# Variance of four chunks as four 32-column products, roots on 128 partitions, the low part on GpSimd, and a share of one scaling on ScalarE

## The reference

```python
x = x + _L0_conv_ref(_gn(x), ...)   # masked, float32
x = x + _L1_conv_ref(_gn(x), ...)   # masked, left and right rounded to bfloat16
x = x + _L2_conv_ref(_gn(x), ...)   # no layer norm ahead, 16 channels
x = x + _L3_conv_ref(_gn(x), ...)   # no mask
```

```python
xn = layernorm(x, norm_g, norm_b)
m = mask[..., None]
left = xn @ Wl.T * m * jax.nn.sigmoid(xn @ Wlg.T)
right = xn @ Wr.T * m * jax.nn.sigmoid(xn @ Wrg.T)
out_gate = jax.nn.sigmoid(xn @ Wog.T)
out = jnp.einsum('bikd,bjkd->bijd', left, right)
out = layernorm(out, out_norm_g, out_norm_b) * out_gate
return out @ Wout.T
```

## Time and profile before

| | |
|---|---|
| median of three runs | 2122.47 us (2121.59 to 2125.39) |
| the profiled execution, its own time | 2120.04 us |
| its span in the profile | 2118.1 us |
| mean granted PE clock, share of full speed | 0.959 |
| busy in the span | PE 1768.2, DVE 1489.3, ACT 1344.1, POOL 805.5 us |
| `project` of layers 0, 1 and 3, gate sigmoids of first to last chunk | 98.4 to 357.2, 697.3 to 967.0, 1536.8 to 1800.9 us |
| `output` of layer 3, first to last scaling | 1970.0 to 2107.4 us |

### The profile page before, as it was taken

How to read it: one execution, slowest core, us unless ns; L and a number is a source line. 1 busy time by engine, 2 the same in 40 slices (tenths; PEclk the granted TensorE clock), 3 DMA queues, 4 the chain that set the end, 5 groups by cost and what they waited for, 6 DMA issues and landing times. The chain is left out here.

```text
span 2118.1 us, 40561 instructions
## 1 busy us (share of the span) xinstructions
PE 1768.2 (83%) x10305; PEld 1040.4 (49%) x10389; DVE 1489.3 (70%) x3176; ACT 1344.1 (63%) x2413; POOL 805.5 (38%) x740
## 2 busy tenths in 40 slices
PE   0899996797998999965599799799799997799665
PEld 0445444685553444443255477644345444688332
DVE  7688886125753999995977388466489899344775
ACT  0587884455995787854599566478487876244322
POOL 0045445005990344445699300089000000000799
PEclk9999998998998999998899899999899999899999
DMA  7367776774995355546399666199456867653799
GB/s 322 132 199 231 246 237 208 284 313 155 365 366 179 121 173 181 175 138 236 132 347 367 234 221 206 43 327 393 150 181 213 263 214 222 248 238 158 258 358 336
DMA packets 326944, 496.13 MB, mean 234 GB/s; under 512 B 22827, under 2 KB 188462, under 8 KB 320438
## 3 DMA queue, kind: packets, MB, share of 16 engines
q1 hardware_dynamic: 326838, 494.93, 68.0%
HBM read 285.12 MB, written 197.13 MB: 228 GB/s over the span
## 5 line engine op out<-in xcount | busy, mean ns | idle before, releaser
L1327 POOL TENSOR_TENSOR shared<-O,out_rs 128x128 f32<-128x128 f32 (+1 forms) x128 | 92.1, 722 | 676.5 <-DVE out_rs L1227 675.5
L601 PE MATMUL ps<-w_heads,hi 64*128 64x256 f16 x3072 | 291.2, 272 | 39.5 <-DVE sig L752 27.2
L664 ACT ACTIVATE sig<-ps,largest 128x512 f32<-128x512 f32 x384 | 247.3, 692 | 51.5 <-PE ps L601 49.6
L1104 ACT ACTIVATE O<-ps 128x512 f32 (+1 forms) x144 | 151.7, 1053 | 189.2 <-PE ps L1025 189.2
L645 ACT ACTIVATE zs<-ps,shift 128x512 f32<-128x512 f32 x192 | 131.8, 686 | 183.3 <-PE ps L569 183.2
L601 PEld LDWEIGHTS ps<-w_heads,hi 64*128 64x128 f16 x3072 | 154.4, 94 | 187.5 <-DVE sig L752 71.5
L1371 PEld LDWEIGHTS ps<-ident,shared 128*128 128x128 f32 (+1 forms) x1024 | 118.8, 134 | 235.9 <-POOL shared L1327 141.5
L1371 PE MATMUL ps<-ident,shared 128*128 128x128 f32 (+1 forms) x1024 | 162.7, 284 | 79.3 <-POOL shared L1327 79.2
L601 PE MATMUL ps<-w_heads,lo 64*128 64x256 f16 x1536 | 212.7, 271 | 0.0
L569 PE MATMUL ps<-xs,center 128*128 128x512 f32 x384 | 202.3, 609 | 11.7 <-DVE r_terms L716 5.4
L752 DVE SCALAR_TENSOR_TENSOR sig<-ps,largest,sig 128x512 f32<-128x512 f32 x256 | 179.6, 742 | 38.0 <-ACT sig L664 36.5
(11 more groups left out here) (163 smaller groups left out, 3642.1 us busy)
## 6 DMA issues: line engine op xcount, KB each, us to landing
shared<-left_right SPq DMA_DIRECT2D x34, 2048.0 KB, 12.1
shared<-gate SPq DMA_DIRECT2D x224, 256.0 KB, 4.5
gate<-gates SPq DMA_DIRECT2D x96, 512.0 KB, 2.9
x_dram<-shared SPq DMA_DIRECT2D x192, 256.0 KB, 4.3
shared<-x_dram SPq DMA_DIRECT2D x192, 256.0 KB, 4.4
xs<-x_dram SPq DMA_DIRECT2D x64, 512.0 KB, 4.2
left_right<-stage SPq DMA_DIRECT2D x64, 448.0 KB, 5.7
left_right<-shared SPq DMA_DIRECT2D x64, 448.0 KB, 5.8
```

What stands on the lines that cost most here:

```text
L601: last = pe.matmul(PAIR[row][:, g, kb * S:kb * S + S], tokens[half, q % 8, at:at + P], k["w_heads"][half, part, :], start=(step == 0), sto ...
L664: act.activation(sig[:, slot, :].rearrange("p (c e) -> p c e", c=4), pair(row, 0), ACT.Sigmoid, scale=k["largest"][:, 0:1]).then_inc(c["si ...
L1104: act.activation(o_of(ch), ps[h % 4 // 2][:, h % 2, :].rearrange("p (b g i) -> p b g i", b=2, g=2), ACT.Copy).then_inc(c["o_copied"].sem, 1)
```

## The change

Three parts.

In `project`, `variance` now works on four chunks at a time: four products with 32 columns each, the first into partitions 0 to 31 of `VAR`, the others into 32, 64 and 96 onwards. Within a batch of eight, the second group of four adds to the first; each group's slice of `var_w` puts its sums three times over into rows of its own. It stands between the centre product and the heads instead of behind the gate product. `root` and `split_r` work on all 128 partitions, and `split_r` makes the three parts with two vectors of -1, 0 in place of slices; the logarithm and the exponential are written to the same tile. `sq` has four slots.

`lo` is made by GpSimd, in layer 3 too. The leads are two chunks shorter, the rings of hi and lo have four slots instead of eight, and the two memsets of `r_terms` are gone.

In `output` of layer 3, ACT scales the last chunk of each batch of four, with eight instructions of 128 x 64; GpSimd scales the other three.

```diff
-R_PART, R_ONE = 32, 96
+QUADS, QUAD, R_ONE = 4, 32, 31
...
-    LOAD, CENTER, VARIANCE, SPLIT, NORM = 16, 14, 13, 5, 4
+    LOAD, CENTER, VARIANCE, SPLIT, NORM = 14, 12, 11, 3, 2
...
-            def variance(i, q):
-                pe.wait_ge(c["sq_done"].sem, c["sq_done"](m + 1))
-                    pe.wait_ge(c["log_done"].sem, c["log_done"](batch))
-                w = k["var_w"][:, 2 * (BATCH - 1 - at):2 * (BATCH - 1 - at) + P]
-                pe.matmul(VAR, w, sq[:, q % 2, :], start=(at == 0), stop=(at == BATCH - 1)).then_inc(c["var_done"].sem, 1)
+            def variance(i, group):
+                pe.wait_ge(c["sq_done"].sem, c["sq_done"](g * QUADS + QUADS))
+                    pe.wait_ge(c["log_done"].sem, c["log_done"](batch))
+                for part in range(QUADS):
+                    last = pe.matmul(VAR[part * QUAD:part * QUAD + QUAD, :], k["var_w"][:, half, :], sq[:, part, :],
+                                     start=(half == 0), stop=(half == BATCH // QUADS - 1))
+                last.then_inc(c["var_done"].sem, 1)
...
                 if more(CENTER):
                     center(i, q + CENTER, Z, i * BODY + q + CENTER)
+                if more(VARIANCE) and (q + CENTER) % QUADS == 0:
+                    variance(i, (q + CENTER) // QUADS - 1)
                 heads(i, q, 0)
                 heads(i, q, 1)
                 out_gate(i, q)
-                if more(VARIANCE):
-                    variance(i, q + VARIANCE)
...
-                act.activation(log_var[:], VAR[0:2 * BATCH, :], ACT.Ln, bias=k["unit"][0:2 * BATCH, 2:3]).then_inc(c["log_done"].sem, 1)
-                act.activation(r[:], log_var[:], ACT.Exp, scale=-0.5).then_inc(c["r_done"].sem, 1)
+                act.activation(r[:], VAR, ACT.Ln, bias=k["unit"][:, 3:4]).then_inc(c["log_done"].sem, 1)
+                act.activation(r[:], r[:], ACT.Exp, scale=-0.5).then_inc(c["r_done"].sem, 1)
...
-                dve.tensor_copy(terms[0], r[:]).then_inc(parts.sem, 1)
-                dve.tensor_tensor(r_rest[:], r[:], terms[0], ALU.subtract).then_inc(parts.sem, 1)
-                dve.tensor_copy(r_mid[:], r_rest[:]).then_inc(parts.sem, 1)
-                dve.tensor_copy(terms[1], r_mid[:])
-                dve.tensor_tensor(terms[2], r_rest[:], r_mid[:], ALU.subtract).then_inc(split.sem, 1)
+                dve.tensor_copy(r_mid[:], r[:]).then_inc(parts.sem, 1)
+                dve.scalar_tensor_tensor(r_rest[:], r_mid[:], k["unit"][:, 4:5], r[:], ALU.mult, ALU.add).then_inc(parts.sem, 1)
+                dve.tensor_copy(r_mid[:], r_rest[:]).then_inc(parts.sem, 1)
+                dve.scalar_tensor_tensor(r_rest[:], r_mid[:], k["unit"][:, 5:6], r_rest[:], ALU.mult, ALU.add).then_inc(parts.sem, 1)
+                dve.tensor_copy(r_terms[:, b % 2, :], r_rest[:]).then_inc(split.sem, 1)
...
-                dve.tensor_tensor(lo[:, q % 8, :], xn[:, q % 2, :], hi[:, q % 8, :], ALU.subtract).then_inc(c["lo_done"].sem, 1)
...
+            def low_part(i, q):
+                m = i * BODY + q
+                pool.wait_ge(c["xn_done"].sem, c["xn_done"](m + 1))
+                pool.wait_ge(c["hi_done"].sem, c["hi_done"](m + 1))
+                pool.tensor_tensor(lo[:, q % 4, :], xn[:, q % 2, :], hi[:, q % 4, :], ALU.subtract).then_inc(c["lo_done"].sem, 1)
...
+    shares_scale = n == 3
...
+            def scaled_by_act(q):
+                return shares_scale and q % BATCH == BATCH - 1
...
-                if not gate_first and more(SCALE):
+                if not gate_first and more(SCALE) and not scaled_by_act(q + SCALE):
                     scale(i, q + SCALE)
...
+            def scale(i, q):
+                m = i * BODY + q
+                act.wait_ge(c["ln_scale"].sem, c["ln_scale"](i * BATCHES + q // BATCH + 1))
+                act.wait_ge(c["wt_done"].sem, c["wt_done"](m - 3))
+                for jb in range(2):
+                    for token in range(2 * ROWS):
+                        tokens = rows[:, jb, bass.ds(m * 2 * ROWS + token, 1), :].rearrange("p t h -> p (t h)")
+                        at = q % BATCH * 2 * ROWS + token
+                        last = act.activation(scaled[:, q % RING, jb, token, :], tokens, ACT.Copy,
+                                              scale=rs[:, q // BATCH % BATCHES, jb, at:at + 1])
+                last.then_inc(c["act_scaled"].sem, 1)
```

More of the change, by code:

```diff
@@ L600, in heads @@
                             half = slice(g * C, g * C + C)
-                            last = pe.matmul(PAIR[row][:, g, kb * S:kb * S + S], tokens[half, q % 8, at:at + P],
+                            last = pe.matmul(PAIR[row][:, g, kb * S:kb * S + S], tokens[half, q % 4, at:at + P],
                                              k["w_heads"][half, part, :], start=(step == 0), stop=(step == 2))
@@ L629, in _ @@
                 center(0, q, AHEAD_Z[q % 2], q - 1)
-                if q > 0:
-                    variance(0, q - 1)
+                if q > 0 and q % QUADS == 0:
+                    variance(0, q // QUADS - 1)
                 for part in between.get(q, ()):
@@ L764, in _ @@
             fold.scale_output(dve)
-            fold.normed_weights(dve, beside=clear_r_terms)
+            fold.normed_weights(dve)
             split_r(0, 0)
@@ new lines, in _, with mask_pair, mask_rows, step @@
+        @block.gpsimd
+        def _(pool):
+            def mask_pair(i, q, row):
+                m = i * BODY + q
+                b = q // SCH
+                if q % SCH == 0 and row == 0:
+                    pool.wait_ge(c[f"lr_out{b}"].sem, c[f"lr_out{b}"](i * 16 * SEG_PARTS))
+                    pool.wait_ge(c[f"first_out{b}"].sem, c[f"first_out{b}"](i * 64))
+                pool.wait_ge(c["pair_read"].sem, c["pair_read"](m * 2 + row + 1))
+                product = sig[:, (2 * q + row) % 4, :].rearrange("p (a e) -> p a e", a=4)
+                by_g = k["mask"][:].rearrange("p g b i -> p (g b) i")
+                mk = by_g[:, :, bass.ds(m * ROWS + row, 1)].to_broadcast([P, 4, P])
+                pool.tensor_tensor(staged(b, q, row), product, mk,
+                                   ALU.mult).then_inc(c["lr_done"].sem, 1)
+            def mask_rows(i, q):
+                m = i * BODY + q
+                b = q // SCH
+                if q % SCH == 0:
+                    pool.wait_ge(c[f"lr_out{b}"].sem, c[f"lr_out{b}"](i * 16 * SEG_PARTS))
+                    pool.wait_ge(c[f"first_out{b}"].sem, c[f"first_out{b}"](i * 64))
+                pool.wait_ge(c["pair_read"].sem, c["pair_read"](m * 2 + 2))
+                slot, at = 2 * q % 4, q % SCH * ROWS
+                product = sig[:, slot:slot + 2, :].rearrange("p r (c e) -> p c e r", c=4)
+                by_g = k["mask"][:].rearrange("p g b i -> p (g b) i")
+                mk = by_g[:, :, bass.ds(m * ROWS, ROWS)].unsqueeze(2).to_broadcast([P, 4, P, ROWS])
+                rows = stage[b].rearrange("p g b l n (h i) -> p (g b) (l n h) i", h=HG)[:, :, :, at:at + ROWS]
+                pool.tensor_tensor(rows, product, mk, ALU.mult).then_inc(c["lr_done"].sem, 2)
+            def low_part(i, q):
+                m = i * BODY + q
+                pool.wait_ge(c["xn_done"].sem, c["xn_done"](m + 1))
+                pool.wait_ge(c["hi_done"].sem, c["hi_done"](m + 1))
+                pool.tensor_tensor(lo[:, q % 4, :], xn[:, q % 2, :], hi[:, q % 4, :], ALU.subtract).then_inc(c["lo_done"].sem, 1)
+            def step(i, q, more):
+                if more(NORM):
+                    low_part(i, q + NORM)
+                if paired:
+                    mask_rows(i, q)
+                elif masked:
+                    for row in range(ROWS):
+                        mask_pair(i, q, row)
+            for q in range(NORM):
+                low_part(0, q)
+            bodies_of(pool, step)
@@ L1426, in step @@
                     copy(i, q + TURN)
+                if more(SCALE) and scaled_by_act(q + SCALE):
+                    scale(i, q + SCALE)
                 if gate_first:
@@ L1462, in output @@
         c["aggregated"].advance(5)
-    for name in ("ln_stat", "scaled", "wt_done", "wt_copied", "out_mm_done", "x_new",
+    c["scaled"].advance(NCH - batches if shares_scale else NCH)
+    if shares_scale:
+        c["act_scaled"].advance(batches)
+    for name in ("ln_stat", "wt_done", "wt_copied", "out_mm_done", "x_new",
                  *(("centered", "gated") if gate_first else ("out_gated",))) + (("counted",) if counted else ()):
@@ L1475, in constants @@
     group = np.arange(P) % C // 2
-    var_w = np.zeros((P, 2 * BATCH - 2 + P), np.float32)
+    halves = BATCH // QUADS
+    var_w = np.zeros((P, halves, QUAD), np.float32)
     spread = np.zeros((P, BATCH, P), np.float32)
-    for g in range(2):
-        half = slice(g * C, g * C + C)
-        var_w[half, 2 * BATCH - 2 + g] = live[half] / C
-        for q in range(BATCH):
-            for part in range(3):
-                spread[R_PART * part + 2 * q + g, q, half] = live[half]
+    third = np.full(QUAD, -1)
```

(11 more changed lines are left out.)

130 lines of the change are left out of this document (53 added, 77 removed).

## The result

| | before | after |
|---|---|---|
| median, 7 runs each | 2122.47 us | 2111.51 us (2107.93 to 2115.64) |
| ratio, 95% interval | | 0.9948 (0.9933 to 0.9963) |
| span of the profiled execution | 2118.1 us | 2106.1 us |
| granted PE clock over the span | 0.959 | 0.928 |

Faster, by 0.5%, where 2.5% was forecast (2069 us). The time lies inside the stated range of 2018 to 2125, but that range reached past no change (2122), so this says little; the sum that led to 2069 was wrong.

What follows compares the result with a forecast made beforehand. PE was taken to bound layer 0's project, DVE layer 1's, GpSimd layer 3's output. Gains of 30.4 (project stages), 11.4 (starts) and 12 (output), 54 us, turned 2120.0 into 2066; 2.4 more gave 2069, range 2018 to 2125.

Steps and rivals of the forecast that it cites:

- shorter leads: Project stages' starts: two norms less before the first heads product save 3.8 us per layer; smaller rings cost nothing.
- The root stall: PE's wait behind ACT's root: 2.58 us at the gate product plus 0.7 for the split, 3.3 in all.
- V: PE time of one group of four 32-column variance products in project, taken as 2.15 us.
- The side-by-side rival: All four variance products of a group run at once on PE, 0.86 us per group, 2019 in all; chance 0.12.
- my sum for the stages: Per project stage: 51 chunks at 3.24, 13 groups, 7 root stalls, last 12 chunks; forecast 254.4 us, layer 3 253.4.
- The last chunks: Project's last 12 chunks, without centre product: 10 at GpSimd's 3.35 us and 2 at PE's 2.3, 38.1 together.
- lo: Its move from DVE to GpSimd in project: 1.27 us each, covered while chunks are still centred, uncovered at the end.
- The starts: Before the first heads product in three project stages: 3.8 us less each, 11.4 together, PE held by nothing else.
- The output: Layer 3's output: each fourth chunk's scaling on ACT takes GpSimd from 2.21 to 1.96 us per chunk; 12 us gained.
- The range: Whole kernel, 2018 to 2125 us; said to leave out 0.18, from the slower no-overlap part and half the lowest case.

Runs made afterwards that it cites:

- e1: The changed kernel with LOAD 16 instead of 14, so x is loaded four chunks ahead of its centre product instead of two; 2042.4 us.
- e2: The changed kernel with the centre product made three times in the step where PE would wait for the gate sigmoid behind a root; 2088.9 us.
- e10: e1 with the centre product made three times, in a step four chunks away from the root's wait, as a control; 2088.3 us.
- e6: e1 with centre product, group, root and split one chunk earlier in relation to the spread that needs the split; 2027.0 us.
- e12: e1 with three more products in each batch's first group, all into the first product's own partitions 0 to 31; 2098.8 us.
- e9: e6 with the centre product made three times in the step where PE would wait for the gate sigmoid behind the root; 2020.6 us.
- e8: e1 with lo back on DVE in the three layers; 2079.8 us.
- e4: The changed kernel with GpSimd doing all scalings of layer 3's output again, as before the change; 2123.7 us.
- e11: e6 with the group of four products behind the gate product of its step instead of ahead of the heads; 2089.9 us.

## Why the prediction went wrong, step by step

- **The step that failed** stands under shorter leads: "The memset pair and the smaller rings cost nothing that a row shows: two chunks of lead are 8 us." It looks at the way from norm to heads alone and prices it at the old chunk; the stage's sum has no term for the loads of x, and none for a granted clock under full speed. Both were put at nothing without a row. LOAD and CENTER both went down by two, so their distance stayed two chunks; but at 3.25 us these are 6.5 us where they were 8.2, with loads that take up to 7.1 to land in layer 0 and a queue that for 16.4 us in every eight chunks issues stores. The rows were there to see before: on SP's queue, the stores' 16.4 us were exactly PE's four chunks. What the runs showed in its place: 37.5 us of waits for x, and with the longer lead of e1 the stages are 65 us shorter.
- **The root stall** was forecast at 3.3, and is 3.2: 2.3 at the gate product (2.58 forecast) and 0.8 at the spread (0.7). Right in mechanism and size, but priced at its idle time alone. On top of it comes the low clock behind it. e2 gets 22.6 us back by giving PE more to do, e10 nothing; e6 takes the split's part.
- **V** was 2.15 and is 1.00: wrong by 39 x 1.15 = 45 us, in the direction that should have made the kernel faster than forecast. That each product's "second must wait for its first" was an argument, not a row, and it doesn't keep four products apart. The side-by-side rival had the mechanism; the Trainium skill ("TensorE: Matmul & The Clock Gate", Part 3, Measured speedup vs the span model), by which a pack takes about one product's time, agrees with 1.00, and in e12 products on the same columns don't pass side by side. By the sum, 45 us more on top of the same losses would have made the kernel slower than before: that it is faster at all is luck as far as this forecast goes, and so is layer 1's 253.2 beside 254.4.
- **With V = 1.00 my sum for the stages is 165.2 + 13.0 + 23.1 + 38.1 = 239.4**, and 238.4 for layer 3: 717 in all. Measured 803, so 86 us are missing from it. The waits for x are 37.5 of them; for the other 49 the low clock is the cause that the rows show, by the estimate above up to 62 us. e1 takes 65 us away. The 13 and 8 us of e6 and e9 bring the stages to 716.9, but that this meets the sum is chance: they come in part out of the root stalls, which the sum had counted. How the 49 divide between the low clock behind x and behind the roots isn't shown exactly.
- **The last chunks** were forecast at 3.35 us each, with GpSimd as the limit. In layer 0 PE waited 0.2 us for lo; five of the chunks passed 2.4 to 2.5 us apart, and then ACT's gate sigmoids waited 4.4 us for slots that the stores of the gate, from SP's queue, hadn't freed. The last twelve periods together took 35.5 us, 38.1 forecast: near in size, with another cause.
- **lo** on GpSimd: 1.16 us, 1.27 forecast; PE waited 0.2 us for it in layer 0 of e1. Right. What its move is worth, e8 says: 37 us with PE as it is (39 by the stages).
- **The starts**: 10.8 us, 11.4 forecast, and the first heads product stands 3.7 us earlier in layer 0, 4 forecast. But "PE being held by nothing else there" was wrong: the split holds PE for 4.50 us in each start. That the size came out is in part luck.
- **The output**: 12.2, 12 forecast, and e4 confirms the cause. GpSimd stays at 20.00 of 20, while the 1.99 us per chunk are near the 1.96 of the forecast. The small scalings take 0.34 us each, over the "at most 0.32". DMA gives 396 to 404 GB/s, above the 358 of the Trainium skill ("SBUF — State Buffer", A bandwidth-pool intuition that's wrong), by which there would have been no gain here.

- **The range** leaves out 0.13 + 0.06 = 0.19, not 0.18, by the prediction's own chances.

So the gain went to a load lead that the shorter chunk made too short, behind an in-order queue, and to the clock behind the stalls.

## What to carry to other kernels

When a stage's period shrinks, go through every lead and every queue and price them at the new period: a distance of n chunks loses n times what the chunk lost (here 2 x 0.85 us), and SP's issuing didn't shrink with it. A wait of PE can cost its length and then the slow products behind it; where one can't be removed, cheap repeated products put exactly there can pay (e2), while four chunks away they only cost (e10). A step that is late by less than one chunk can be moved by a chunk, after checking which ring its reader empties (e6 against e11). And a view of waits over the whole kernel mixes a stage's start with its loop: divide by what stands in the loop.

## What the runs showed that I hadn't expected

- Four float32 products on four sets of 32 columns pass in 1.00 us, one alone in 0.86, although each has two records; on the same columns each takes 0.85.
- 31 us of extra float32 products made the kernel 22.6 us faster.
- SP takes 1.7 us to issue one store of a part (6.72 for four) where a load of x takes it 0.34 to 1.05.
- Removing waits of 37.5 us removed 65 us.
